# Order of the first chunks on VectorE and ScalarE: sums and transposes ahead of the layer-norm moments

## The reference

```
h = relu(layernorm(x))                        # mean and variance over the 128 features
d = 1/sqrt(sum(adj, axis=-1))
z = leaky_relu(d * (adj @ (d * h)) @ W1 + b1, 0.1)
S = exp(-sqrt(pairwise squared distances of z + 1e-10) / 2), only the 4 best of each row kept
A2 = S + adj ;  d2 = 1/sqrt(rowsum(A2))
x  = x + d2 * (A2 @ (d2 * h)) @ W2 + b2
h  = relu(layernorm(x))
x  = x + h @ W_self.T + (adj @ h) @ W_neigh.T + b
```

## Time and profile before

| | us |
|---|---|
| median of 3 runs | 1301.8 (1300.81 to 1305.67) |
| profiled execution | 1301.95 |
| its span, first to last instruction | 1300.3 |
| VectorE / ScalarE / POOL / TensorE busy | 867.5 / 597.6 / 661.7 / 938.8 |

### The profile page before, as it was taken

How to read it: one execution, slowest core, us unless ns; L and a number is a source line. 1 busy time by engine, 2 the same in 40 slices (tenths; PEclk the granted TensorE clock), 3 DMA queues, 4 the chain that set the end, 5 groups by cost and what they waited for, 6 DMA issues and landing times.

```text
span 1300.3 us, 13534 instructions
## 1 busy us (share of the span) xinstructions
PE 938.8 (72%) x3570; PEld 665.8 (51%) x3570; DVE 867.5 (67%) x843; ACT 597.6 (46%) x1105; POOL 661.7 (51%) x937
## 2 busy tenths in 40 slices
PE   0133163465668899899999994577777777799998
PEld 0111031232233444477777773455666666588886
DVE  0955474455444321279999999947777777788785
ACT  0533342354442321255555555535555554567673
POOL 9798877877830000044444444588888887200000
PEclk9975676886888899899999998798888888899999
DMA  9999999999998874295444445695777777599993
GB/s 222 323 348 370 361 346 366 360 365 366 345 363 319 307 255 171 73 269 210 157 155 155 158 156 203 186 385 209 276 284 270 280 275 273 216 362 381 378 378 127
DMA packets 115653, 357.73 MB, mean 275 GB/s; under 512 B 34464, under 2 KB 59808, under 8 KB 87456
## 3 DMA queue, kind: packets, MB, share of 16 engines
q1 hardware_dynamic: 59296, 273.11, 55.1%
q0 software_dynamic: 47104, 80.00, 20.6%
q10 hardware_dynamic: 9216, 4.20, 1.2%
HBM read 250.02 MB, written 106.95 MB: 275 GB/s over the span
## 4 chain that ended last, share of the span: by engine, by line
PE 40%; POOL 19%; DMA 19%; issue 10%; DVE 7%; ACT 2%; SPq 1%; POOLq 0%; ACTq 0%; DVEq 0%
DMA araw<-in_adj_dram 16%; POOL zt_lo L567 11%; PE ps L1138 7%; POOL araw L350 7%; PE ps L1227 5%; PE ps L1230 5%; PE ps L1228 5%; PE ps L1229 5%; PE ps L1250 4%; PE ps L1251 4%; PE ps L1252 4%; DVE part L872 2%; DVE tr L857 1%; DMA hw_scratch<-z_st 1%; DMA xs<-in_x_dram 1%
## 5 line engine op out<-in xcount | busy, mean ns | idle before, releaser
L350 POOL DMA_DIRECT2D araw<-in_adj_dram x512 | 302.2, 599 | 65.6 <-ACTq L628 25.2
L999 DVE TENSOR_TENSOR araw_r<-araw,tr_r 128x2048 fp32r<-128x2048 f32 x128 | 289.8, 2297 | 45.9 <-ACT tr_r L722 45.5
L722 ACT ACTIVATE tr_r<-araw 128x2048 fp32r<-128x2048 f32 x128 | 241.8, 1911 | 67.4 <-PE ps L1252 41.5
L567 POOL DMA_INDIRECT zt_lo<-neighbour_table,idx_st x128 | 197.2, 1541 | 45.7 <-issue 40.0
L705 ACT ACTIVATE araw<-ps,nsq 128x1024 f32<-128x1024 f32 x128 | 142.8, 1117 | 113.3 <-PE ps L1230 90.7
L1250 PE MATMUL ps<-araw_r,zt_hi 128*128 128x512 f32 x256 | 110.9, 433 | 90.1 <-issue 33.7
L624 ACT ACTIVATE ps<-araw 128x256 f32<-128x256 f32 x304 | 111.4, 367 | 65.0 <-DMA araw<-in_adj_dram 61.5
L872 DVE TENSOR_REDUCE part<-araw 128x16 f32<-128x4096 f32 x13 | 57.4, 4414 | 97.4 <-DMA araw<-in_adj_dram 97.4
L1227 PE MATMUL ps<-sq_rows,pick 128*128 128x512 f32 x256 | 102.2, 399 | 17.1 <-ACT araw L705 9.5
L1250 PE MATMUL ps<-araw_r,ys_r 128*128 128x512 f32 x256 | 101.7, 397 | 9.3 <-DVE araw_r L999 9.3
L1250 PEld LDWEIGHTS ps<-araw_r,zt_hi 128*128 128x128 f32 x256 | 52.6, 205 | 106.6 <-issue 65.5
(11 more groups left out here) (150 smaller groups left out, 1632.6 us busy)
## 6 DMA issues: line engine op xcount, KB each, us to landing
araw<-transposed SPq DMA_DIRECT2D x156, 1024.0 KB, 5.1
araw<-in_adj_dram POOLq DMA_DIRECT2D x512, 128.0 KB, 20.7
keys_scratch<-araw SPq DMA_DIRECT2D x64, 512.0 KB, 4.3
transposed<-tr SPq DMA_DIRECT2D x28, 1024.0 KB, 8.2
transposed<-unit_zt_hi SPq DMA_DIRECT2D x12, 1024.0 KB, 9.1
transposed<-unit_zt_lo SPq DMA_DIRECT2D x12, 1024.0 KB, 9.8
transposed<-unit_sq_rows SPq DMA_DIRECT2D x12, 1024.0 KB, 9.4
xs<-in_x_dram SPq DMA_DIRECT2D x64, 64.0 KB, 2.0
```

The costliest lines, as they stand in the source:

```text
L350: gp.dma_start(araw[R * q + first:R * q + R:SPREAD, c], adj_v[q, first:R:SPREAD, g // 2, g % 2, :, c]).then_inc(a_first_in[c], DMA)
L567: gp.indirect_dma_start(out=gath[:, i, u, k, :], out_offset=None, in_=table, in_offset=bass.IndirectOffsetOnAxis(ap=idx_st[:, i, u * TOPK ...
L722: act.activation(ring_hi[:, place % TSLOTS], ring[:, j], ACT.Copy).then_inc(hi_done, 1)
L999: v.tensor_tensor(ring_lo[:, j], ring[:, j], ring_hi[:, place % TSLOTS].bitcast(F32), ALU.subtract).then_inc(lo_done, 1)
```

## The change

VectorE: the moments and what follows them become a function `moments()`, called inside the chunk loop after the third chunk of group 0 (`n == CHUNKS - 2`). Ahead of it now stand the two transposes of chunk 0, the reduction and the two transposes of chunk 1 and the two transposes of chunk 2. ScalarE: the row sums of chunks 0 and 2 of group 0 now stand ahead of the root, of `normalize(0)` and of the weight copies. The number of instructions and the data that they handle stay as they are.

```diff
         @block.scalar
-            act.wait_ge(var_ready, 1)
-            act.activation(tmp32[:], tmp32[:], ACT.Sqrt).then_inc(sqrt_done, 1)
-            act.wait_ge(ln_ready, 1)
             def normalize(g):
             ...
-            normalize(0)
-            act.wait_ge(wt_mm, 1)
-            act.activation(ws_t[:], ps_z[:, 0:F], ACT.Copy).then_inc(wt_ev, 1)
-            act.activation(wn_t[:], ps_z[:, F:2 * F], ACT.Copy).then_inc(wt_ev, 1)
...
+            row_sums(0, 0)
+            row_sums(0, 2)
+            act.wait_ge(var_ready, 1)
+            act.activation(tmp32[:], tmp32[:], ACT.Sqrt).then_inc(sqrt_done, 1)
+            act.wait_ge(ln_ready, 1)
+            normalize(0)
+            act.wait_ge(wt_mm, 1)
+            act.activation(ws_t[:], ps_z[:, 0:F], ACT.Copy).then_inc(wt_ev, 1)
+            act.activation(wn_t[:], ps_z[:, F:2 * F], ACT.Copy).then_inc(wt_ev, 1)
+
             for g in range(GROUPS):
-                row_sums(g, 0)
                 if g >= 1:
+                    row_sums(g, 0)
                     keep_partial(g - 1)
                 ht_copy(g)
                 if act_sums(g, 1):
                     row_sums(g, 1)
                 if g == 0:
                     normalize(1)
-                row_sums(g, 2)
+                else:
+                    row_sums(g, 2)
                 root(g)
...
         @block.vector
-            v.wait_ge(x_in, X_IN)
-            for t in range(TILES):
-                ins = v.bn_stats(out=stats[:, t], in_=xs[:, t])
-            ...
+            def moments():
+
+                v.wait_ge(x_in, X_IN)
+                for t in range(TILES):
+                    ins = v.bn_stats(out=stats[:, t], in_=xs[:, t])
+                link(ins)
+                for t in range(TILES):
+                    ins = v.bn_aggr(out=mv[:, t], in_=stats[:, t])
+                link(ins)
+                v.tensor_scalar(tmp32[:], mv[:, :, 1], LN_EPS, None, ALU.add).then_inc(var_ready, 1)
+                v.wait_ge(sqrt_done, 1)
+                link(v.reciprocal(tmp32[:], tmp32[:]))
+                v.scalar_tensor_tensor(negmr[:], mv[:, :, 0], -1.0, tmp32[:], ALU.mult, ALU.mult).then_inc(ln_ready, 1)

             for n, (g, c) in enumerate(part_a):
...
                     if late_diag(g - 1, j):
                         make_y(g - 1)
+                if n == CHUNKS - 2:
+                    moments()
                 if c == CHUNKS - 1:
```

## The result

| | median us (runs) | ratio to before, 95% interval |
|---|---|---|
| before | 1308.85 (22) | |
| after | 1302.57 (22) | 0.9955 [0.9939, 0.9970] |

The change wins 5.9 us, between 3.9 and 8.0. The forecast was 2.0 us, its range reached to 8. The level of before is 7 us above the median of the three runs shown first; ratios here are always against runs of before on the same chip.

What follows compares the result with a forecast made beforehand. The prediction took the first pass to be held by full DMA engines except in a hole behind POOL's stop; closing it wins 2.0 us, 1301.95 - 2.0 = 1299.95, said as 1299.9, own range 1298 to 1302, with rivals 1293.6 to 1304.4.

Steps and rivals of the forecast that it cites:

- the 2.0 of the sum: First pass: DMA time not full, 1.9 us in 50 to 54 us plus 0.2 in 42 to 50, taken as 2.0.
- rival A: First pass: POOL's lead in issuing loads is kept, so its whole 8.2 us stop is won, 1293.8 us; 14%.
- the step had 2.0: First pass: closing the DMA hole behind POOL's stop wins 2.0 us, bounds 0 to 8.2.
- The term that failed: First pass, 8 to 42 us: DMA share already 1.08, so early stores win nothing there.
- My sign of a wrong prediction: DMA share full at 50-54 us yet last reduction unmoved or 5 us earlier, or stages behind the pass change length.
- the step had allowed 5: VectorE, group 0: chunk 0's two stores queue ahead of chunk 2, some 5 us, so it lands between 39.1 and 44.1.
- Rival B: End of first pass: last two chunks land close together, VectorE late by 4.4 us at most, 1304.4 us; 12%.
- Rival C: First pass: the hole comes back elsewhere, VectorE without a unit from 48.6 to 63 us; 1301.95, no change; 6%.
- Rival D: ScalarE's longer list before the h copies delays groups 0 and 1 until POOL waits over 17 us; 3%.
- Rival E: First pass: VectorE's work holds POOL's issues back, losing 17.9 us against 8.2 won, 1311.7 us; 3%.

Runs made afterwards that it cites:

- dve_only: Changed order on VectorE alone, ScalarE's block as in the kernel before; ratio to before 1.0072, 9.4 us slower.
- late_stores: Changed kernel with SyncE held before its first store until five units are transposed, run twice; ratios to before 0.9980 and 0.9984.
- act_chunk0: Kernel before with only ScalarE's sums of chunk 0 moved ahead of its wait for the variance; ratio to before 0.9996.
- moments_early: Changed kernel with the moments one chunk earlier, after chunk 1; ratio to before 0.9957.
- pool_first: Changed kernel with POOL's first load issues ahead of its five affine_selects; ratio to before 0.9953.
- wide_start: Changed kernel with POOL's first loads ahead of its affine_selects and ScalarE issuing 16 of 32 x loads; ratios to before 0.9920 and 0.9946.
- three_issuers: POOL-first, split-x kernel with group 0's chunk 1 issued by SyncE and chunk 2 by ScalarE, ahead of their x halves; ratio to before 0.9974.
- after_again: The changed kernel unedited, run a second time; ratio to before 0.9959, 5.4 us gained.

## Why the prediction was right, and where it was not

*The number.* 1302.57 us against the 1299.9 forecast looks close, and part of that is luck: the level of before had been read 7 us too low, from three runs, the gain set some 4 us too small, and the two errors partly cancel. The gain of 5.9 us is three times the 2.0 of the sum, and lies nearer to the 8.2 of rival A. It stays under the 6.5 us below which the prediction expects hardly to tell a difference by only 0.6 us, and with 22 runs of each it was told.

*Bound and hole: right.* The pass hangs on the DMA engines, the stop of POOL drained them, the change closes it. With the early stores held back the gain was 2.7 us, where the step had 2.0. That POOL's stop as such is not the price (rival A's mechanism, though its number came near) is shown from both sides: halving it won 0.5 to 1.3 us where 4.2 us of stop went, and dve_only paid 9.4 us for 20.5 us more.

*The term that failed.* "From 8 to 42 us the share is 1.08 already, so the early stores win nothing there." I set this term at 0; late_stores against after measures 3.5 us in the timed runs, and 1.5 us by the bytes of the traces. I had read the busy share as a measure of work done, though the same row has only 263 GB/s beside its 1.08. With loads alone it stood at 1.06 and 293 GB/s, with stores beside the same loads at 1.04 and 375 (382 and 360 in the other two traces of after). Megabytes moved in 0 to 80 us, against the mean of the two traces of before (288.5 GB/s), and divided by the 360 GB/s of the steady pass; beside it the same count for 0 to 380 us (before: 130.74 MB):

| | GB/s, 0 to 80 us | gain by bytes to 80, us | MB, 0 to 380 us | gain by bytes to 380, us | gain measured, us (95%) |
|---|---|---|---|---|---|
| act_chunk0 | 301 | 2.8 | 131.59 | 2.4 | 0.5 (-1.7 to 2.7) |
| late_stores | 301, 301 | 2.8 | 131.68, 131.79 | 2.6, 2.9 | 2.6 and 2.1 (-0.3 to 5.1) |
| after | 310, 308, 306 | 4.8, 4.3, 3.9 | 132.15, 132.63, 132.01 | 3.9, 5.3, 3.5 | 5.9, 5.4 and 7.2 (3.0 to 9.7) |
| moments_early | 308 | 4.3 | 132.62 | 5.2 | 5.6 (3.0 to 8.4) |
| pool_first | 311 | 5.0 | 132.39 | 4.6 | 6.2 (3.1 to 9.0) |
| wide_start | 326, 325 | 8.3, 8.1 | 133.40, 133.70 | 7.4, 8.2 | 10.5 and 7.1 (4.5 to 14.3) |
| three_issuers | 286 | -0.6 | 130.76 | 0.1 | 3.4 (1.0 to 5.8) |
| dve_only | 261 | -6.1 | 127.55 | -8.8 | -9.4 (-12.6 to -6.3) |

The order is right but for three_issuers. The count to 80 us lies within the measured interval for five of the eight kernels, just outside for act_chunk0 and dve_only, and off by 1.6 us beyond it for three_issuers; the count to 380 us lies within it for all but three_issuers. What is won in the first 80 us is thus still there at the end of the pass. By the DMA share instead of the bytes, 0 to 80 us would give dve_only -8.8 us and late_stores 2.7, both well, but after only 1.9 to 2.7 and wide_start 4.2 to 5.0. This is a count that agrees, not a mechanism: loads and stores need not cost the same per byte, and it treats them alike. For the early stores alone it gives 1.5 us, from traces that spread by 1.8 us among themselves; the 3.5 of the timed runs (standard error 0.7) is not accounted for by it.

*What stays open.* The traces show 2.8 us less at the end of the pass for after (mean of three against mean of two), 4.2 by the bytes to 380 us and 3.2 at the first distance matmul, while the timed runs show 6. My sign of a wrong prediction, that the stages behind the pass change their length, can't be decided by them: from the last reduction to the first distance matmul it is 146.5 to 147.8 us in all fourteen traces, but the distances and what follows them took 757.4 and 757.2 us in the traces of before and 763.2, 760.8 and 762.3 in those of after, and their length goes with the clock as said above. Within each kernel the faster runs have the higher mean granted clock (correlation -0.66 over 117 runs of before, -0.62 over 46 of after), and after's runs have 0.8848 of full clock in the mean, those of before 0.8817, those of late_stores 0.8822. A fit with one slope for the three kernels puts after 3.3 us under before at equal clock, late_stores 2.2; the remaining 2.8 us of after go along with the clock. Whether the early stores raise the clock, by moving TensorE's later stretches in time, or both have another cause, no run here tells.

*Times on the way.* First transposes 20.85 us (forecast 21) and first store 23.2 (23), both right; chunk 1 taken up at 30.8 (31), by the reduction, so that the second pair of transposes began at 35.1. Chunk 2 landed at 45.9, later than the 39.1 to 44.1 given, so group 0's last chunk was done at 68.7 and not by 67.2, and POOL waited 2.06 us at chunk (1,0)'s slot and not 1.2. Chunk 2 came 6.8 us later than the 39.1 without stores ahead of it, where the step had allowed 5, and the moments began at 50.4, after the 44 to 49 given. POOL's wait cost nothing that shows: the DMA share was 1.04 over 60 to 80 us.

*Rival B* was wrong in form and right about the place. VectorE was never late at the end; the last chunk's landing moves by itself. From the last reduction of group 6 to that of group 7 it was 42.4 and 46.3 us in the traces of before, 41.7, 50.0 and 51.3 in those of after. In after_again chunk 3 of the last group came 15.7 us after chunk 2, with VectorE waiting:

```profile
378.88 4.50 DVE L847 STREAM_TRANSPOSE tr<-araw 128x2048 f32<-128x2048 f32 x2 [2.65 <-DMA araw<-in_adj_dram]
394.56 4.42 DVE L876 TENSOR_REDUCE part<-araw 128x16 f32<-128x4096 f32 x1 [11.17 <-DMA araw<-in_adj_dram]
```

After_again stood 8 us ahead of before at the end of group 6 (344.55 against 352.75 and 352.43) and 2.4 ahead of the mean at the last reduction. By the bytes to 380 us it was 5.3 us ahead. So the last reduction, on which the forecast had set its mark, is a poor mark for a few us, and the end of one group is no better. The argument against B, that landings are 9.4 us or more apart as the issues are, was wrong already in the profile before, where the last two came 5.8 us apart.

*Rival C* (the hole comes back) did not happen. *Rival D* (ScalarE's longer list makes POOL wait longer than the queue is deep) did not either: POOL waited 2.1, 2.2 and 3.8 us for ScalarE's sums of chunk (1,0) in the three traces of after, far under 17. *Rival E* (VectorE holds POOL's issues back) is shown wrong. The same line as the earlier trace rows, over the whole span of after, with seven transposes and reductions of VectorE now beside the first issues:

```profile
L350 POOL DMA_DIRECT2D araw<-in_adj_dram x512: 596/598/862, 3.8 to 367.8; - x171
```

128 issues took 75.75 us, 0.592 each, as before the change.

## What to carry to other kernels

A DMA share of 1.0 says that the engines have something to do, not how much they move: set GB/s beside it, and where one kind of transfer runs alone at a lower rate, ask what would start the other kind sooner. Where a buffer has two consumers on two engines, both must be moved ahead: VectorE's part alone made this kernel 9 us slower. And a difference of 0.5% needs the timed runs: here single traces showed half of it or the reverse, and the bytes moved by a late time told more than the place of any one landing.

## What the runs showed that I had not expected

- Loads alone ran at 293 GB/s with a share of 1.06, loads and stores together at 360 to 382 GB/s with 1.04.
- Issuing the same 16 adjacency loads took 1.74 us each on SyncE and 0.59 on POOL; SyncE's x loads took 0.44 in the median before the change.
- The first pass of an unchanged kernel ended at 395.1 in one execution and at 398.8 in another. The distance search behind it took 253 us in both, and 255 to 257 us in eleven of the twelve traces of the other kernels, where the granted clock dipped.
